# RWKV state exponentials: two clamps on GpSimd in place of two Relu passes on ScalarE, with a new order on all engines

## The chip, the cores and the metric

The kernel runs on one core of one Trainium2 chip. The metric is the device time of that core in microseconds, lower is better. The engines are called as in the profile: PE (TensorE, matrix multiplies), DVE (VectorE), ACT (ScalarE, the table functions), POOL (GpSimd) and SP (the queue that issues the transfers). Everything is float32.

## The reference

The input is 16 sequences of 512 tokens with 128 channels. Four blocks follow one another: a four-layer RWKV model with a residual, a feed-forward block with weights and activations rounded to FP4 in blocks of 16, a causal attention with one head, and the same feed-forward block again. Cut to what matters here:

```python
x = x + rwkv_model(_layernorm(x))      # 4 layers, each: time mix, then channel mix
x = x + fp4_ffn(_layernorm(x))
x = x + attention(_layernorm(x))
x = x + fp4_ffn(_layernorm(x))

def step(carry, kv):                   # the RWKV state, one token
    aa, bb, pp = carry
    kk, vv = kv
    ww = u + kk
    qq = jnp.maximum(pp, ww)
    e1 = jnp.exp(pp - qq)
    e2 = jnp.exp(ww - qq)
    out = (e1 * aa + e2 * vv) / (e1 * bb + e2)
    ww2 = pp + w                       # w = -exp(time_decay)
    qq2 = jnp.maximum(ww2, kk)
    e1b = jnp.exp(ww2 - qq2)
    e2b = jnp.exp(kk - qq2)
    return ((e1b * aa + e2b * vv, e1b * bb + e2b, qq2), out)
```

The two exponentials that carry the state forward are `e1b` and `e2b`. With `d = kk - pp` their arguments are `-relu(d - w)` and `-relu(w - d)`.

## The kernel before

Channels lie on the 128 partitions and the 512 tokens of one sequence along the free axis for the RWKV part, so one job is a 128x512 tile. There are 64 RWKV jobs `r` (4 layers by 16 sequences), 32 feed-forward jobs (16 for each of the two blocks) and 16 attention jobs. The running maximum, the denominator and the numerator of the state are three scans along the tokens on DVE (`scan_pp`, `scan_bb`, `scan_aa`).

The program is a software pipeline written out by hand. Each engine has one loop over ticks `t`, and the body of the loop is a list of stage functions, each called with its own lag, such as `exp_k(t - 6)`. A function does nothing when its job number is outside the range. So the order of one engine's instructions is that of its list, an engine works strictly in that order, and semaphores hold an instruction until what it reads has been made or what it overwrites has been read. Nothing else sets the order. A steady RWKV tick carries one instance of each RWKV stage, for some thirteen different jobs at once. RWKV jobs enter in ticks 0 to 63. `FFN_AT`, `ATT_AT` and `FFN2_AT` are the ticks in which the first feed-forward, attention and second feed-forward jobs enter: 69, 85 and 97 (`GAP` is 12). In the ticks in which attention and the second feed-forward overlap, both kinds of stage run.

The stages that the change touches, in job `r`: `scan_pp` makes the running maximum from the keys in PSUM, `sub_d` (DVE, L331) makes `d`, `args` (ACT, L818 and L819) makes both Relu arguments in `ed`, `exp_d` (L825) turns the first into a decay factor in PSUM bank T, `exp_k` (L830) turns the second into the weight of the new key, and `mul_s1`, `scan_bb`, `scan_aa` on DVE use them. Then POOL adds (`add_den` L649, `add_num` L655), ACT makes the seed of a reciprocal (`seeds`, L841), POOL multiplies (`scaled_p` L666, `mul_y` L660), and DVE finishes (`mul_u`, `rwkv`). POOL also makes the roots of the layer norms (`rsqrts`, L601 to L606) and differences of neighbouring tokens (`sub_dh1` L643, `sub_dh` L673), and adds the channel mix to `X` (`add_xb` L678). In a steady tick POOL runs eleven instructions. Six instructions of DVE in a tick read two tiles of SBUF: `mix_t` L307, `mix_rt` L314, `mix_k` L404, `mix_r` L411, `gated` L381 and `rwkv` L387.

## Time and profile before

| what | value |
|---|---|
| three runs, median (lowest to highest) | 1396.85 us (1396.58 to 1397.21) |
| profiled execution, span | 1396.8 us |
| PE busy | 1311.6 us, 94% |
| ACT busy | 1261.8 us, 90% |
| DVE busy | 1250.5 us, 90% |
| POOL busy | 1160.8 us, 83% |
| mean granted TensorE clock | 0.989 |

The span of the profiled execution is its own time from the first to the last instruction, and it stands at the median of the runs, so sums made against the span need no conversion. The shares of busy time are means over very different stretches: up to about 855 us the RWKV ticks, then the first feed-forward, from about 1106 us attention alone, from about 1180 us attention and the second feed-forward together, and from about 1279 us the second feed-forward alone. An instruction's duration in the trace holds some latency under which its successor already starts, so the time that an instruction takes from its engine is the distance from its start to the next start; such distances are called spacings below.

### The profile page before, as it was taken

The numbers are of one execution on the slowest core, as the hardware profiler recorded it, in microseconds if no ns is written. First come the engines' busy times: TensorE is split into PE (matmuls) and PEld (weight loads), VectorE is DVE, ScalarE is ACT, GpSimd is POOL, SyncE is SP. The second block draws the span as 40 slices with busy tenths as digits, with TensorE's granted clock in tenths as the row PEclk, the third lists the DMA queues.
The fourth block names the chain that finished last, engine by engine and source line by source line (L and its number), as shares of the span: only waits on it lengthen the run. The fifth ranks groups of instructions, "written<-read, shape, count | busy, mean of one in ns | idle before, by whom it ended". The sixth has DMA issues, their size and how long they took to land.

```text
span 1396.8 us, 23610 instructions
## 1 busy us (share of the span) xinstructions
PE 1311.6 (94%) x7285; PEld 929.9 (67%) x7285; DVE 1250.5 (90%) x2169; ACT 1261.8 (90%) x2533; POOL 1160.8 (83%) x1218
## 2 busy tenths in 40 slices
PE   3699999999999999999999999999999999999997
PEld 1356667666666666676666677766667777667776
DVE  6999999999999999999999999579999467789994
ACT  6799999999999999999999999767777889888874
POOL 6888999999998999998998999969998445467983
PEclk9999999999999999999999999999999999999999
DMA  7000000000000000000000000100000000000011
GB/s 232 0 1 1 1 1 1 1 20 13 1 1 1 1 1 1 1 1 1 1 2 0 1 1 9 31 24 23 24 1 1 1 1 1 1 8 23 24 31 38
DMA packets 26924, 18.55 MB, mean 13 GB/s; under 512 B 1072, under 2 KB 26160, under 8 KB 26800
## 3 DMA queue, kind: packets, MB, share of 16 engines
q1 hardware_dynamic: 26800, 17.05, 4.2%
q8 instruction: 59, 0.97, 0.3%
q14 instruction: 65, 0.53, 0.1%
HBM read 12.85 MB, written 4.19 MB: 12 GB/s over the span
## 4 chain that ended last, share of the span: by engine, by line
ACT 40%; PE 30%; issue 11%; POOL 10%; DVE 8%; DMA 0%; ACTq 0%; SPq 0%; POOLq 0%; DVEq 0%
ACT z L757 10%; ACT kf L867 6%; PE ps L1211 5%; ACT kf L874 3%; PE ps L1190 3%; ACT rc L841 3%; PE ps L1152 3%; ACT ed L818 3%; PE ps L1183 3%; PE ps L1261 3%; PE ps L1135 3%; ACT er L835 2%; PE ps L1243 2%; ACT ed L819 2%; ACT ed L830 2%
## 5 line engine op out<-in xcount | busy, mean ns | idle before, releaser
L1152 PEld LDWEIGHTS ps<-W,kf 128*128 128x128 f32 x2048 | 245.9, 193 | 33.1 <-issue 32.3
L1135 PE MATMUL ps<-xk,W 128*128 128x512 f32 x512 | 262.5, 595 | 1.0 <-DVE xk L404 0.9
L1152 PE MATMUL ps<-W,kf 128*128 128x128 f32 x2048 | 251.2, 276 | 0.0
L757 ACT ACTIVATE z<-X,ln_rs 128x128 f32<-128x128 f32 x512 | 219.2, 720 | 6.1 <-POOL ln_rs L606 6.1
L867 ACT ACTIVATE kf<-ps 128x512 f32<-128x512 f32 x256 | 210.8, 823 | 3.5 <-PE ps L1135 3.5
L874 ACT ACTIVATE kf<-kf 128x1024 f32<-128x1024 f32 x128 | 164.7, 1287 | 0.0
L1040 PEld LDWEIGHTS ps<-idn,z 128*128 128x128 f32 x664 | 81.1, 143 | 113.7 <-issue 68.4
L1040 PE MATMUL ps<-idn,z 128*128 128x128 f32 x664 | 101.9, 277 | 32.8 <-ACT z L757 19.4
L604 POOL TENSOR_TENSOR ln_rs<-ln_rs,mhalf 128x8 f32<-128x8 f32 (+1 forms) x70 | 122.9, 1756 | 0.0
L707 POOL TENSOR_TENSOR W<-W,hsc 128x704 f32<-128x704 f32 x64 | 88.9, 1389 | 30.3 <-DVE hsc L482 30.3
L666 POOL TENSOR_TENSOR p<-p,rc 128x512 f32<-128x512 f32 x64 | 104.2, 1628 | 8.6 <-DVE p L381 8.0
L673 POOL TENSOR_TENSOR dh<-h 128x512 f32<-128x512 f32 x64 | 66.8, 1044 | 48.4 <-ACT h L860 48.2
L1190 PE MATMUL ps<-WU,d 128*128 128x352 f32 x256 | 99.9, 472 | 5.5 <-DVE W L463 4.8
L1183 PE MATMUL ps<-WG,d 128*128 128x352 f32 x256 | 97.6, 463 | 0.6 <-ACT d L898 0.6
L358 DVE TENSOR_TENSOR_SCAN bb<-ps,ed 128x512 f32<-128x512 f32 x64 | 78.3, 1223 | 19.5 <-ACT ed L830 19.4
L713 POOL TENSOR_TENSOR W<-W,hsc 128x704 f32<-128x704 f32 x64 | 88.8, 1388 | 2.6 <-DVE W L494 2.5
L226 DVE BATCH_NORM_STATS2 ln_st<-X 128x6 f32<-128x256 f32 x256 | 90.5, 413 | 0.1
L1122 PEld LDWEIGHTS ps<-W,rc 128*128 128x128 f32 x512 | 67.0, 191 | 33.8 <-issue 33.8
L1142 PEld LDWEIGHTS ps<-W,xc 128*128 128x128 f32 x512 | 64.3, 191 | 36.5 <-ACT sr L810 24.8
L649 POOL TENSOR_TENSOR er<-er,bb 128x512 f32<-128x512 f32 x64 | 81.4, 1273 | 2.3 <-DVE bb L358 2.3
L655 POOL TENSOR_TENSOR rv<-rv,aa 128x512 f32<-128x512 f32 x64 | 81.5, 1273 | 1.4 <-DVE aa L366 1.3
L678 POOL TENSOR_TENSOR X<-X,cr 128x512 f32<-128x512 f32 x64 | 81.5, 1273 | 0.0
(178 smaller groups left out, 4041.5 us busy)
## 6 DMA issues: line engine op xcount, KB each, us to landing
X<-x_in SPq DMA_DIRECT2D x16, 256.0 KB, 6.8
xi<-x_in SPq DMA_DIRECT2D x16, 256.0 KB, 2.8
out<-X SPq DMA_DIRECT2D x16, 256.0 KB, 2.3
W<-weights SPq DMA_DIRECT2D x4, 832.0 KB, 8.4
W<-fp4w SPq DMA_DIRECT2D x1, 560.0 KB, 3.6
row<-rows SPq DMA_DIRECT2D x1, 192.0 KB, 2.9
wqkv<-qkv SPq DMA_DIRECT2D x1, 96.0 KB, 5.9
idn<-ident SPq DMA_DIRECT2D x1, 64.0 KB, 3.0
```

The costliest lines, as they stand in the source:

```text
L226: last = e.bn_stats(g.of(g.st, n)[:, 2 * k:2 * k + 2, :].rearrange("p a s -> p (a s)"), src[:, k * 256:(k + 1) * 256].rearrange("p (a c) - ...
L604: e.tensor_tensor(rs[:, 0, :], rs[:, 2, :], mhalf[:, 0:k], ALU.pow).then_inc(*own.next())
L666: e.tensor_tensor(p[r % 2][:, :], p[r % 2][:, :], rc[r % 2][:, :], ALU.mult).then_inc(ps_done, 1)
L707: e.tensor_tensor(h, h, spread(hsc[n % 2][:, 0, k * 44:(k + 1) * 44], 44), ALU.mult).then_inc(fh_y[k], 1)
L757: last = e.activation(chunk(dst, j), chunk(src, j), ACT.Identity, bias=rs[:, 1, j:j + 1], scale=rs[:, 0, j:j + 1])
L867: e.activation(kf[r % 3][:, f, :], (pF0, pF1)[f % 2][:, :], ACT.Relu).then_inc(relu_done[f], 1)
L874: e.activation(both, both, ACT.Square).then_inc(sq_done[k], 1)
L1040: last = e.transpose(chunk(dst, j), chunk(src, j), idn[:, :])
L1135: e.matmul((pF0, pF1)[f % 2][:, :], w_of(r, WCK + f), xk[r % 2][:, :], start=True, stop=True).then_inc(kf_mm[f], 1)
L1152: last = e.matmul(chunk(pKV, j), kf[r % 3][:, f, j * 128:(j + 1) * 128], w_of(r, WCV + f), start=f == 0 and j == 0, stop=f == 3, skip_grou ...
L1183: e.matmul(pG[j % 2][:, 0:I], chunk(fx[n % 2], j), WG[:, :], start=True, stop=True).then_inc(g_mm, 1)
L1190: e.matmul(pU[j % 2][:, 0:I], chunk(fx[n % 2], j), WU[:, :], start=True, stop=True).then_inc(u_mm, 1)
```

## The change

ACT no longer makes the arguments. `args` is gone, and POOL gets two functions. `clamp_old` writes `max(d, -ew)` (`ew` is `exp(time_decay)`, `wneg` its negative), `clamp_new` writes `min(d, -ew)`. The second operation of each is there only because the form takes two, with a bound of 3e38. The two exponentials now add the constant back as a bias read per partition: `exp(-(max(d, -ew)) - ew)` and `exp(min(d, -ew) + ew)`. One semaphore for the arguments becomes two. Arithmetic, tiles, matmuls and transfers are otherwise the same.

```diff
+FAR = 3e38
...
-GAP = 12
-ATT_AT, FFN2_AT, TICKS = FFN_AT + NB, FFN_AT + NB + GAP, FFN_AT + 2 * NB + GAP + 18
+ATT_AT, FFN2_AT = FFN_AT + 16, FFN_AT + 33
+TICKS = FFN2_AT + 35
...
             def sub_d(r):
                 if 0 <= r < NR:
-                    w.wait_ge(args_done, r - 1)
+                    w.wait_ge(old_done, r - 1)
+                    w.wait_ge(new_done, r - 1)
...
+            def clamp_old(r):
+                if 0 <= r < NR:
+                    w.wait_ge(wneg_done, 1)
+                    w.wait_ge(ed_done, r - 1)
+                    w.wait_ge(d_done, r + 1)
+                    e.tensor_scalar(ed[r % 2][:, 0, :], dd[r % 2][:, :], FAR, col(wneg, r), ALU.min, ALU.max).then_inc(old_done, 1)
+
+            def clamp_new(r):
+                if 0 <= r < NR:
+                    w.wait_ge(wneg_done, 1)
+                    w.wait_ge(s1_done, r - 1)
+                    w.wait_ge(bb_done, r - 1)
+                    w.wait_ge(d_done, r + 1)
+                    e.tensor_scalar(ed[r % 2][:, 1, :], dd[r % 2][:, :], col(wneg, r), -FAR, ALU.min, ALU.max).then_inc(new_done, 1)
...
-            def args(r):
-                if 0 <= r < NR:
-                    w.wait_ge(wneg_done, 1)
-                    w.wait_ge(s1_done, r - 1)
-                    w.wait_ge(bb_done, r - 1)
-                    w.wait_ge(d_done, r + 1)
-                    e.activation(ed[r % 2][:, 0, :], dd[r % 2][:, :], ACT.Relu, bias=col(ew, r))
-                    e.activation(ed[r % 2][:, 1, :], dd[r % 2][:, :], ACT.Relu, bias=col(wneg, r), scale=-1.0).then_inc(args_done, 1)
-
...
-                    w.wait_ge(args_done, r + 1)
-                    e.activation(pT[:, :], ed[r % 2][:, 0, :], ACT.Exp, scale=-1.0).then_inc(ed_done, 1)
+                    w.wait_ge(old_done, r + 1)
+                    e.activation(pT[:, :], ed[r % 2][:, 0, :], ACT.Exp, bias=col(wneg, r), scale=-1.0).then_inc(ed_done, 1)
...
-                    w.wait_ge(args_done, r + 1)
-                    e.activation(ed[r % 2][:, 1, :], ed[r % 2][:, 1, :], ACT.Exp, scale=-1.0).then_inc(ek_done, 1)
+                    w.wait_ge(new_done, r + 1)
+                    e.activation(ed[r % 2][:, 1, :], ed[r % 2][:, 1, :], ACT.Exp, bias=col(ew, r)).then_inc(ek_done, 1)
...
             for t in range(TICKS):
-                add_num(t - 7)
...
+                rsqrts(t - 2)
+                scaled_p(t - 6)
...
```

The four lists of stages, on DVE, POOL, ACT and PE, are all written anew, with other lags. `FFN_AT` and `ATT_AT` keep their values, 69 and 85; `FFN2_AT` goes from 97 to 102.

POOL, one steady RWKV tick of the program before. `dh` is both differences, `er` and `rv` the denominator and the numerator, `p` the gated output, `ln_rs` the roots:

```order
L673 TENSOR_TENSOR dh<-h 128x512
L601 TENSOR_SCALAR ln_rs<-ln_st 128x8
L602 TENSOR_SCALAR ln_rs<-ln_st 128x8
L604 TENSOR_TENSOR ln_rs<-ln_rs,mhalf 128x8
L606 TENSOR_TENSOR ln_rs<-ln_rs 128x8
L666 TENSOR_TENSOR p<-p,rc 128x512
L660 TENSOR_TENSOR er<-er,rc 128x512
L678 TENSOR_TENSOR X<-X,cr 128x512
L643 TENSOR_TENSOR dh<-h 128x512
L649 TENSOR_TENSOR er<-er,bb 128x512
L655 TENSOR_TENSOR rv<-rv,aa 128x512
```

POOL, the steady tick of the changed program, from the denominator on. L660 and L652 are the clamps:

```order
L666 TENSOR_TENSOR er<-er,bb 128x512
L672 TENSOR_TENSOR rv<-rv,aa 128x512
L660 TENSOR_SCALAR ed<-d,wneg 128x512
L652 TENSOR_SCALAR ed<-d,wneg 128x512
L690 TENSOR_TENSOR dh<-h 128x512
L603 TENSOR_SCALAR ln_rs<-ln_st 128x8
L604 TENSOR_SCALAR ln_rs<-ln_st 128x8
L606 TENSOR_TENSOR ln_rs<-ln_rs,mhalf 128x8
L608 TENSOR_TENSOR ln_rs<-ln_rs 128x8
L683 TENSOR_TENSOR p<-p,rc 128x512
L645 TENSOR_TENSOR dh<-h 128x512
```

Thirteen instructions stand in a tick where eleven stood. The clamps come straight ahead of the channel-mix difference and the roots, and behind the numerator.

DVE, the part of the steady tick with the instructions that read two tiles of SBUF, before:

```order
L373 SCALAR_TENSOR_TENSOR p<-ps,p 128x512
L331 TENSOR_TENSOR d<-ps,pp 128x512
L387 SCALAR_TENSOR_TENSOR rc<-er,p 128x512
L314 SCALAR_TENSOR_TENSOR sr<-dh,vec,h 128x512
L337 TENSOR_SCALAR er<-d,vec 128x512
L411 SCALAR_TENSOR_TENSOR xc<-dh,vec,h 128x512
L404 SCALAR_TENSOR_TENSOR xk<-dh,vec,h 128x512
L381 SCALAR_TENSOR_TENSOR p<-sr,rv 128x512
L307 SCALAR_TENSOR_TENSOR xt<-dh,vec,h 128x512
```

The same part of the changed program:

```order
L333 TENSOR_TENSOR d<-ps,pp 128x512
L375 SCALAR_TENSOR_TENSOR p<-ps,p 128x512
L227 BN_STATS ln_st<-X 128x6 x2
L389 SCALAR_TENSOR_TENSOR rc<-er,p 128x512
L383 SCALAR_TENSOR_TENSOR p<-sr,rv 128x512
L339 TENSOR_SCALAR er<-d,vec 128x512
L406 SCALAR_TENSOR_TENSOR xk<-dh,vec,h 128x512
L308 SCALAR_TENSOR_TENSOR xt<-dh,vec,h 128x512
L315 SCALAR_TENSOR_TENSOR sr<-dh,vec,h 128x512
L413 SCALAR_TENSOR_TENSOR xc<-dh,vec,h 128x512
```

The six still stand together with one other instruction among them. Between `d` and the first of them there are now two instructions, where there was none.

ACT, where the second feed-forward meets attention, in the program before. `er` is the SiLU of the feed-forward, `big` and `kf` with `sm` the exponentials of the softmax. The last such place but one:

```order
L983 ACTIVATE kf<-ps 128x384
L941 ACTIVATE X<-ps 128x512
L976 ACT_TABLE_LOAD
L976 ACTIVATE big,sm<-ps,sm 128x128
L983 ACTIVATE kf<-ps 128x256
```

The changed program where the first SiLU of the second feed-forward comes:

```order
L776 ACTIVATE z<-X,ff_rs 128x128 x4
L987 ACTIVATE big,sm<-ps,sm 128x512
L917 ACT_TABLE_LOAD
L917 ACTIVATE er<-ps 128x352
L994 ACTIVATE kf<-ps 128x512
```

Over the whole program the table loads go from 14 to 4: the last softmax exponential now stands ahead of the first SiLU of the second feed-forward, and they no longer alternate.

## Rows read from the trace of the kernel before

**Rows 1.** Busy time by engine in two stretches: 40 RWKV ticks, and attention overlapping feed-forward.
```profile
core 0: us, PE busy (x) PEld busy (x) DVE busy (x) ACT busy (x) POOL busy (x), PEclk, DMA share, GB/s
177.90:705.70 527.80, 527.25 (x2879) 361.75 (x2878) 510.15 (x801) 527.80 (x1001) 482.59 (x442) 1.00 0.01 3
...
1180.00:1279.00 99.00, 89.73 (x518) 65.75 (x519) 79.70 (x181) 84.24 (x187) 57.89 (x64) 1.00 0.02 6
```

**Rows 2.** Timeline of POOL: start, duration, then idle time before in brackets.
```profile
407.20 1.04 POOL L673 TENSOR_TENSOR dh<-h 128x512 f32<-128x512 f32 x1 [0.90 <-ACT h L860]
...
420.40 1.04 POOL L673 TENSOR_TENSOR dh<-h 128x512 f32<-128x512 f32 x1 [0.90 <-ACT h L860]
421.52 0.52 POOL L601 TENSOR_SCALAR ln_rs<-ln_st 128x8 f32<-128x8 f32 x1
422.12 0.62 POOL L602 TENSOR_SCALAR ln_rs<-ln_st 128x8 f32<-128x8 f32 x1
422.71 1.85 POOL L604 TENSOR_TENSOR ln_rs<-ln_rs,mhalf 128x8 f32<-128x8 f32 x1
424.64 0.39 POOL L606 TENSOR_TENSOR ln_rs<-ln_rs 128x8 f32<-128x8 f32 x1
425.05 1.72 POOL L666 TENSOR_TENSOR p<-p,rc 128x512 f32<-128x512 f32 x1
```

**Rows 3.** Timeline of ACT in the same tick, around the two argument passes.
```profile
422.26 0.97 ACT L867 ACTIVATE kf<-ps 128x512 f32<-128x512 f32 x1
422.74 1.10 ACT L818 ACTIVATE ed<-d,ew 128x512 f32<-128x512 f32 x1
423.35 1.10 ACT L819 ACTIVATE ed<-d,wneg 128x512 f32<-128x512 f32 x1
423.96 1.16 ACT L803 ACTIVATE h<-ps,vec 128x512 f32<-128x512 f32 x1
```

**Rows 4.** Longest wait of PE's weight loads beside a matmul group, 200 to 800 us.
```profile
PEld ps L1142 <- ACT sr L810: 24.3, 39, 0.7
```

**Rows 5.** POOL groups: shape and count, then busy us, mean ns.
```profile
L707 POOL TENSOR_TENSOR W<-W,hsc 128x704 f32<-128x704 f32 x64 | 88.9, 1389 | 30.3 <-DVE hsc L482 30.3
...
L655 POOL TENSOR_TENSOR rv<-rv,aa 128x512 f32<-128x512 f32 x64 | 81.5, 1273 | 1.4 <-DVE aa L366 1.3
...
L694 POOL TENSOR_TENSOR z<-z,xsc 128x512 f32<-128x512 f32 x22 | 23.6, 1075 | 16.3 <-DVE xsc L442 16.3
...
L601 POOL TENSOR_SCALAR ff_rs<-ff_st 128x4 f32<-128x4 f32 x32 | 6.3, 197 | 8.2 <-DVE ff_st L226 5.6
```

**Rows 6.** Timeline of DVE in the tick of rows 2 and 3: first two, last.
```profile
421.24 0.74 DVE L387 SCALAR_TENSOR_TENSOR rc<-er,p 128x512 f32<-128x512 f32 x1
421.90 0.74 DVE L314 SCALAR_TENSOR_TENSOR sr<-dh,vec,h 128x512 f32<-128x512 f32 x1
...
424.89 0.74 DVE L307 SCALAR_TENSOR_TENSOR xt<-dh,vec,h 128x512 f32<-128x512 f32 x1
```

**Rows 7.** Timeline of DVE: the same line in two neighbouring ticks, later.
```profile
721.29 0.68 DVE L393 TENSOR_TENSOR X<-X,ps 128x512 f32<-128x512 f32 x1
...
733.80 0.68 DVE L393 TENSOR_TENSOR X<-X,ps 128x512 f32<-128x512 f32 x1
```

**Rows 8.** Timelines of DVE and ACT: ticks of attention, of both, of feed-forward.
```profile
1139.82 1.13 DVE L527 SCALAR_TENSOR_TENSOR X<-ps,sm,X 128x128 f32<-128x128 f32 x4 [1.07 <-PE ps L1261]
1147.50 1.13 DVE L527 SCALAR_TENSOR_TENSOR X<-ps,sm,X 128x128 f32<-128x128 f32 x4 [0.41 <-PE ps L1261]
...
1222.71 1.11 DVE L527 SCALAR_TENSOR_TENSOR X<-ps,sm,X 128x128 f32<-128x128 f32 x4
1238.66 1.12 DVE L527 SCALAR_TENSOR_TENSOR X<-ps,sm,X 128x128 f32<-128x128 f32 x4
...
1297.98 0.60 ACT L941 ACTIVATE X<-ps 128x512 f32<-128x512 f32 x1
1307.87 0.60 ACT L941 ACTIVATE X<-ps 128x512 f32<-128x512 f32 x1
```

**Rows 9.** ACT groups: table loads of the softmax exponential and of SiLU.
```profile
L906 ACT ACT_TABLE_LOAD x7 | 9.0, 1283 | 5.7 <-PE ps L1183 5.7
L976 ACT ACT_TABLE_LOAD x6 | 7.7, 1283 | 0.1
```

More of the change, by code:

```diff
@@ L573, in vector @@
[L573 to L584 removed]
+                mix_r(t - 12)
+                mul_rv(t - 7)
+                fh_add(ffn_job(t - 8), 0)
@@ new lines, in vector @@
+                mul_up(ffn_job(t - 7), 3)
+                mul_s1(t - 7)
+                fh_sub(ffn_job(t - 8), 0)
+                fh_max(ffn_job(t - 7))
+                scan_bb(t - 7)
+                scan_aa(t - 7)
+                a_add(att_job(t - 9))
+                fh_add(ffn_job(t - 8), 1)
+                fh_scale(ffn_job(t - 7))
+                fx_max(ffn_job(t - 3))
+                fh_inverse(ffn_job(t - 7))
+                add_xa(t - 9)
+                gate(t - 13)
+                mul_up(ffn_job(t - 6), 0)
@@ new lines, in vector @@
+                fh_sub(ffn_job(t - 8), 1)
+                scan_pp(t - 6)
+                prepare(t - 4)
+                a_mask(att_job(t - 7), 0)
+                bn2(t - 9)
+                sub_d(t - 6)
+                a_max(att_job(t - 7), 0)
+                a_mask(att_job(t - 7), 1)
+                fx_scale(ffn_job(t - 3))
+                weights_scales(t - Q_AT + 4)
+                a_max(att_job(t - 7), 1)
+                f_bn(ffn_job(t))
+                mul_u(t - 8)
+                bn1(t - 3)
@@ new lines, in vector @@
+                rwkv(t - 8)
+                a_inverse(att_job(t - 8))
+                a_mask(att_job(t - 7), 2)
+                mul_up(ffn_job(t - 6), 1)
+                gated(t - 7)
+                arg_r(t - 6)
+                a_max(att_job(t - 7), 2)
+                init_stats(t - 1)
+                mix_k(t - 10)
+                mix_t(t - 5)
+                a_mask(att_job(t - 7), 3)
+                fx_add(ffn_job(t - 4))
+                mix_rt(t - 5)
+                a_bn(att_job(t - 3))
@@ new lines, in scalar @@
+                put_x(ffn_job(t - 8))
+                f_z(ffn_job(t - 1))
+                tanh_c(t - 11)
+                init_z(t - 1)
+                seeds(t - 6)
+                a_exp(att_job(t - 6), 3)
+                exp_k(t - 5)
+                exp_r(t - 5)
+                keep_h1(t - 3)
+                relu(t - 10, 3)
+                silu(ffn_job(t - 4), 0)
+                a_z(att_job(t - 3))
+                exp_d(t - 5)
+                keep_av(att_job(t - 5))
+                fh_magic(ffn_job(t - 6), 1)
@@ new lines, in scalar @@
+                keep_hq(ffn_job(t - 7), 1)
+                keep_hq(ffn_job(t - 7), 0)
+                tanh_r(t - 5)
+                norm2(t - 8)
+                weights_out(t - Q_AT - 14)
+                keep_x(ffn_job(t - 8))
+                norm1(t - 2)
+                relu(t - 9, 0)
+                keep_pt(att_job(t - 6), 0)
+                square(t - 10, 0)
+                square_1(t - 6)
+                keep_pt(att_job(t - 6), 1)
+                relu(t - 9, 1)
+                a_exp(att_job(t - 5), 0)
@@ new lines, in tensor @@
+                ff_keys(t - 11, 3)
+                turn1(t - 4)
+                lend_M(ffn_job(t - 6), 0)
+                h_turn(ffn_job(t - 8), 0)
+                ff_values(t - 12, 1)
+                receptance(t - 6)
+                h_turn(ffn_job(t - 8), 1)
+                lend_T(t - 6)
+                down(ffn_job(t - 9))
+                similarity(att_job(t - 6), 0)
+                h_turn(ffn_job(t - 8), 2)
+                lend_M(ffn_job(t - 6), 1)
+                p_turn(att_job(t - 7), 0)
```

226 lines of the change are left out of this document (71 added, 155 removed).

## The prediction

> **What bounds the kernel now.** I read the busy time by stretch first, because the shares over the whole span mix four kinds of work. Over 40 steady RWKV ticks (527.80 us, so 13.20 us each) ACT is busy for all of the stretch and PE for all but half a microsecond, DVE has about 0.44 us idle in a tick and POOL about 1.13 us [rows 1]. Then I read the timelines of one such tick. POOL repeats after 13.20 us with one idle piece of 0.90 us ahead of the channel-mix difference, so its list takes 12.30 us as it stands [rows 2]. ACT starts one pass as the spacing of the last is over: it is the bound, and its list is 13.20 us long. PE is close behind it. Its busy time is modelled, so I look at what its weight loads wait for: those of L1142 wait for ACT 39 times, 24.3 us, or 0.62 us a tick [rows 4], part of it under the matmul ahead. So PE's own list lies between 12.6 and 13.2 us; I take 13.1, since its busy row shows almost no hole. DVE's own list I read where it has fallen behind and runs without a hole: 12.51 us from tick to tick [rows 7]. So the four lists are, in order, ACT 13.2, PE 13.1, DVE 12.5, POOL 12.3. Whatever shortens ACT alone can give 0.1 us a tick before PE ends it, and POOL has room for 0.9 us.
>
> **What goes from ACT.** The two argument passes have spacings of 0.61 us each, 1.22 us a tick [rows 3]. The two exponentials get a bias per partition. No row shows an exponential with and without one; the bound is nothing from below, and from above the difference between the biased Relu (0.61) and the unbiased Relu of L867 (0.48), 0.13 us each. I take the upper end, since the nearest row is also an ACT pass over 512 columns: ACT falls to 13.20 - 1.22 + 0.26 = 12.2 us a tick and is no longer a bound.
>
> **What comes to POOL.** Two clamps a tick. The trace has no one-input POOL instruction on 512 columns, so this is the cost to bound. From below: a one-input instruction on 4 columns takes 0.197 us, which is nearly all fixed cost [rows 5]. From above: the two-input addition on the same shape, 1.27 us long, with a spacing of some 1.24. Between them, the products with a spread factor are 1.389 us for 704 columns and 1.075 for 512 [rows 5], so 0.314 us for 192 columns, 1.64 ns a column for two inputs. If a POOL instruction is paced by what it reads, one input costs half of that, 0.42 us for 512 columns, and with the fixed 0.2 the clamp takes about 0.6 us. I take 0.60; the ends 0.20 and 1.24 stay for the range.
>
> The Trainium skill says on this, in "GPSIMD Engine Reference", section 3.1, that a body of one or two operations runs at 1.03 cycles an element, and that the best a general loop has shown is 768 ns for 512 elements. The first would give 0.44 us plus the fixed part, the second 0.77 us plus it; no row here shows either. By the second the sum would be some 0.35 us a tick worse than mine.
>
> POOL's list becomes 12.30 + 2 x 0.60 = 13.50 us, if it loses as much to DVE as now. That is 0.30 us more than the tick of before. The idle 0.90 us [rows 2] covers three quarters of the clamps and the rest is on the path, because POOL then never rests. I count 51 ticks in which this holds: the 40 of [rows 1] and 11 more up to 855 us. 51 x 0.30 = 15.3 us more.
>
> **What POOL loses to DVE.** POOL and DVE side by side show a second cost [rows 2, 6]. The first root instruction L601 takes 0.52 us here and the same line takes 0.197 us on half the columns in the feed-forward. It starts at 421.52, while DVE's L387, which reads two tiles of SBUF, runs to 421.98, and it ends just after that. L602 (0.62) ends as DVE's L314 ends. The product L666 takes 1.72 us against 1.27 for its like L655; it starts under DVE's L307. So POOL waits while DVE reads two SBUF tiles: 0.32 for L601, about 0.4 for L602, 0.45 for L666, and a little in the others, some 1.5 us of its 12.3. What keeps this small is where the six such DVE instructions stand: from 421.24 to 425.6 they lie over the roots, which read eight columns.
>
> The Trainium skill states a rule for this, in "SBUF — State Buffer", section "Who interferes with whom": a DVE instruction with two SBUF inputs and a POOL instruction that reads SBUF share a read interface, and the one that comes first holds it to its end. The trace agrees on POOL's side (1.72 against 1.27). The rule speaks against this change, because each clamp is one more SBUF read on POOL.
>
> In the new order the clamps can't start before `d`, and behind `d` DVE has only `mul_u` and a pair of statistics, about 1.25 us, before the six begin. POOL needs 2 x 0.60 + 1.0 for the clamps and the difference L690 before it is at the roots. So the roots come about 1 us after the six have begun, and one or two of these fall on a POOL instruction with 512 columns. Bounds: the loss falls by all of its 1.5 us, or the first two of the six add their length, 0.6 each, to it. I take no difference, since the roots still lie under four of the six.
>
> **The other waits.** `clamp_new` waits for `d`; behind it on POOL stand the other clamp, the difference and the roots, for which ACT's two norms and then PE's transposes wait. If `d` is late all of that is late, but POOL, as the bound, should be late itself. The exponentials have most of a tick until DVE needs them. `sub_d` waits for the clamps of two jobs back and never does. These I cost at nothing; if they are not hidden, each gap on POOL is worth its length in every tick. Matmuls and transfers are the same in number and kind, and SP's queue is untouched.
>
> **The opening.** Ticks of before with the input norm in them are longer. ACT gets 1 us a tick there but PE has the mixes of the first ten jobs as further matmuls and POOL its clamps. Between 5 us gained and 5 lost over those ticks; I take 2 gained.
>
> **The tail.** Ten of 14 table loads go; at 1283 ns each [rows 9] that is 12.8 us of ACT. A tick of attention alone takes 7.68 us, a tick of both 15.95, and a tick of feed-forward alone 9.89 [rows 8]. Overlapping saves 7.68 + 9.89 - 15.95 = 1.6 us for each pair, and the changed program gives up some five such pairs, 8 us lost. Against it stand the emptying and filling ticks between the two, which are shorter than full ones, and the table loads: PE is busy for 89.73 of 99 us in the overlap [rows 1], so up to 9.3 us can be got back there. The ends are 8 us lost and 12.8 gained; I take 5 us gained, since ACT's loads stand on the way of SiLU, for which DVE waits.
>
> **Sum.** Against the span of 1396.8 us, which is the median of the runs (1396.85): 1396.8 + 15.3 - 2 - 5 = 1405.1 us.
>
> **Rivals.**
> - *The clamps fit (faster).* If two clamps take no more than POOL's idle 0.9 us, or the loss to DVE falls by 0.3 us or more, PE is the bound at 13.1. For it: the order keeps the six DVE instructions together, as it would have to. Against it: it needs 0.45 us a clamp, hardly more than half the reading of a two-input product with almost no fixed part. Time: 1396.8 - 51 x 0.1 - 2 - 5 = 1384.7 us. Chance 0.30.
> - *The cost cancels.* A tick of 13.3 to 13.35 us, 51 x 0.13 = 6.6 us, is what the opening and the tail give. Time: 1396.4 us. Chance 0.12.
> - *POOL and DVE take turns (much slower).* The clamps and L690 fall under the first two of the six and push the roots out from under the rest. It decides once POOL starts a 512-column read later than about 1 us after `d`. Both wait in turn, 0.6 us more a tick: 51 x 0.9 = 45.9 us, time 1396.8 + 45.9 - 7 = 1435.7 us. For it: the 1 us above, and that DVE's own slack is only 0.7 us. Chance 0.12.
> - *A clamp costs what a two-input addition does.* POOL at 12.30 + 2 x 1.24 = 14.78, 51 x 1.58 = 80.6 us, time 1470 us. Chance 0.04.
> - The forecast, POOL the bound at 13.50 us: chance 0.42, with its own range of 1397 to 1418 us (13.35 to 13.75 a tick).
>
> **How the numbers follow.** A measurement of this kernel tells 0.2%, 2.8 us, from no change. Faster is the first rival and a little of the second, 0.31. Within 0.2% is most of the second and the low edge of the forecast, 0.13. The rest is slower, 0.56. The range must hold eight in ten and cases of both signs: it starts at 1384, the first rival's own time, which leaves out some 0.12 for an opening and a tail that give their most, and ends at 1436, the time of the rival of turns, which leaves out the last rival and a little more, about 0.08.
>
> **What would show it.** In the steady ticks of the changed profile: the tick by POOL's starts should be 13.5 us with no idle piece on POOL, the clamps about 0.64 us long, 0.60 in spacing; ACT should be idle for about 1.3 us a tick; the difference ahead of the roots may be longer than 1.04 us. In the tail, 4 table loads, and attention ticks of 7.7 us up to the end of attention. The forecast is wrong if POOL shows idle time in the steady ticks, if the tick is at or under 13.2 us, or if a clamp is over 0.8 us long.

## The result and the profile after

The changed kernel takes 1443.06 us (median of 4 runs, 1441.99 to 1443.67) against 1396.71 us of the kernel before on the same chip: 1.033 times as long, interval 1.0316 to 1.0345. The forecast was 1405 us, the range ended at 1436. The direction was right and the size was not.

The span went from 1396.8 to 1442.3 us, 45.5 us more. I cut it by the starts of DVE's residual addition (L393 before, L395 after), which stands once in each of the 64 RWKV jobs:

| stretch | before | after | difference |
|---|---|---|---|
| start to the 13th addition | 217.25 | 238.50 | +21.3 |
| 13th to 46th, 33 steady ticks | 435.68 | 452.86 | +17.2 |
| 46th to 64th, in which the second set of weights is prepared | 231.74 | 249.91 | +18.2 |
| 64th to the end | 512.1 | 501.0 | -11.1 |

A steady tick is 13.72 us, 0.52 more than before. Over the 51 steady ticks of the prediction that is 26.6 us; 21.3 lie in the opening, some 9 between the 46th and the 64th addition on top of the steady ticks' own 0.52, and the tail gave 11.1 back.

The first view is the busy time by engine, from the page and for 480 us of steady ticks (35 of them), to be set beside [rows 1].

```profile
PE 1332.3 (92%) x7285; PEld 944.6 (65%) x7285; DVE 1328.8 (92%) x2169; ACT 1194.5 (83%) x2395; POOL 1258.0 (87%) x1346
```

```profile
core 0: us, PE busy (x) PEld busy (x) DVE busy (x) ACT busy (x) POOL busy (x), PEclk, DMA share, GB/s
211.06:691.36 480.30, 466.93 (x2522) 323.90 (x2521) 480.30 (x701) 429.28 (x806) 470.92 (x456) 1.00 0.01 3
```

ACT has come off the bound (1.46 us idle a tick), as intended. DVE is busy for 480.30 of 480.30 us and POOL seems to have 0.27 us a tick free. Both readings mislead. POOL's 0.27 us is the time between the end of one record and the start of the next, none of it a wait; and DVE fills its time only because some of its instructions are long. The timelines show it. First POOL, one steady tick, the answer to [rows 2]: start, duration, and no idle piece in brackets anywhere.

```profile
415.81 1.26 POOL L677 TENSOR_TENSOR er<-er,rc 128x512 f32<-128x512 f32 x1
...
419.49 1.28 POOL L672 TENSOR_TENSOR rv<-rv,aa 128x512 f32<-128x512 f32 x1
420.88 0.68 POOL L660 TENSOR_SCALAR ed<-d,wneg 128x512 f32<-128x512 f32 x1
421.56 0.69 POOL L652 TENSOR_SCALAR ed<-d,wneg 128x512 f32<-128x512 f32 x1
422.21 1.47 POOL L690 TENSOR_TENSOR dh<-h 128x512 f32<-128x512 f32 x1
423.66 0.63 POOL L603 TENSOR_SCALAR ln_rs<-ln_st 128x8 f32<-128x8 f32 x1
424.37 0.35 POOL L604 TENSOR_SCALAR ln_rs<-ln_st 128x8 f32<-128x8 f32 x1
424.70 2.11 POOL L606 TENSOR_TENSOR ln_rs<-ln_rs,mhalf 128x8 f32<-128x8 f32 x1
426.89 0.45 POOL L608 TENSOR_TENSOR ln_rs<-ln_rs 128x8 f32<-128x8 f32 x1
427.30 1.27 POOL L683 TENSOR_TENSOR p<-p,rc 128x512 f32<-128x512 f32 x1
...
429.53 1.26 POOL L677 TENSOR_TENSOR er<-er,rc 128x512 f32<-128x512 f32 x1
```

The line repeats after 13.72 us. A clamp costs 0.68 and 0.65 us from start to start. The first also starts 1.39 us after L672, where such an addition otherwise takes 1.23, so there is 0.15 us more between the addition and the clamp. What makes it isn't shown: the same change of form, from a difference to a root instruction, had 1.12 us behind the 1.04 us long L673 in the kernel before, and has 1.45 behind the 1.47 us long L690 here. Two clamps take 0.68 + 0.65 + 0.15 = 1.48 us. [Rows 2] had 12.30 us of work; 12.30 + 1.48 = 13.78, and 13.72 was measured.

DVE beside it, the answer to [rows 6]:

```profile
421.75 1.04 DVE L389 SCALAR_TENSOR_TENSOR rc<-er,p 128x512 f32<-128x512 f32 x1
422.71 1.52 DVE L383 SCALAR_TENSOR_TENSOR p<-sr,rv 128x512 f32<-128x512 f32 x1
424.15 0.47 DVE L339 TENSOR_SCALAR er<-d,vec 128x512 f32<-128x512 f32 x1
```

L389 ends 0.54 us after the clamp L652 has ended (422.79 against 422.25), L383 0.55 us after the difference L690 (424.23 against 423.68): each waited for POOL's instruction and then ran. Undisturbed they take about 0.7 us, as in [rows 6]. Here it is DVE that waits for POOL, the other way round than in [rows 6]. L690 in turn takes 1.47 us where it took 1.04, and L683 takes 1.27 where its like took 1.72 [rows 2]: these two nearly cancel on POOL.

ACT in the same tick answers to [rows 3]; the second fence is the list of waits from 200 to 800 us (engine and line, whom it waits for, us in all, times, longest).

```profile
422.48 0.73 ACT L840 ACTIVATE ed<-ed,ew 128x512 f32<-128x512 f32 x1
424.66 0.63 ACT L845 ACTIVATE er<-er 128x512 f32<-128x512 f32 x1 [1.45 <-DVE er L339]
...
426.33 0.69 ACT L835 ACTIVATE ps<-ed,wneg 128x512 f32<-128x512 f32 x1
426.95 0.59 ACT L829 ACTIVATE sr<-ps 128x512 f32<-128x512 f32 x1
```

```profile
ACT er L845 <- DVE er L339: 61.5, 42, 2.5
...
PE ps L1095 <- DVE xt L308: 19.0, 42, 2.2
```

ACT and PE, the tightest two before, now wait in every tick; PE's wait for ACT of [rows 4] is gone. L835 has a spacing of 0.62 us with the bias; the same pass without one had 0.54 in the kernel before (L825), and so has L831, shown under the order alone below. So the bias costs 0.08 us. The prediction said that no row shows this pair, but the trace of the kernel before has it: the seeds' exponential L841 reads a bias and has a spacing of 0.61 us.

### The profile page after: what moved, and what is told of

It reads as the page before. It is cut to its first block, busy times and chain, and to the rows that moved or that the text cites. A ratio compares the mean times of both kernels' runs of the same rounds, so it can differ in the third digit from the quotient of the medians.

```text
span 1442.3 us, 23756 instructions
## 1 busy us (share of the span) xinstructions
PE 1332.3 (92%) x7285; PEld 944.6 (65%) x7285; DVE 1328.8 (92%) x2169; ACT 1194.5 (83%) x2395; POOL 1258.0 (87%) x1346
## 4 chain that ended last, share of the span: by engine, by line
DVE 41%; PE 27%; POOL 15%; issue 13%; ACT 3%; DVEq 0%; DMA 0%; POOLq 0%; SPq 0%; ACTq 0%
PE ps L1221 5%; DVE aa L368 4%; DVE pp L324 4%; PE ps L1200 4%; PE ps L1193 3%; DVE ln_st L227 3%; DVE rc L389 3%; PE ps L1209 3%; DVE p L383 3%; PE ps L1253 2%; PE ps L1271 2%; POOL ln_rs L606 2%; DVE rv L346 2%; DVE sr L315 2%; DVE xk L406 2%
## 5 line engine op out<-in xcount | busy, mean ns | idle before, releaser
L776 ACT ACTIVATE z<-X,ln_rs 128x128 f32<-128x128 f32 x512 | 204.3, 488 | 21.2 <-POOL ln_rs L608 21.2
L877 ACT ACTIVATE kf<-ps 128x512 f32<-128x512 f32 x256 | 150.3, 587 | 3.1 <-PE ps L1145 2.8
L606 POOL TENSOR_TENSOR ln_rs<-ln_rs,mhalf 128x8 f32<-128x8 f32 (+1 forms) x70 | 136.1, 1944 | 0.0
L884 ACT ACTIVATE kf<-kf 128x1024 f32<-128x1024 f32 x128 | 135.1, 1057 | 0.0
L1145 PEld LDWEIGHTS ps<-xk,W 128*128 128x128 f32 x512 | 88.3, 194 | 65.9 <-issue 59.4
L845 ACT ACTIVATE er<-er 128x512 f32<-128x512 f32 x64 | 40.3, 630 | 79.3 <-DVE er L339 79.3
L690 POOL TENSOR_TENSOR dh<-h 128x512 f32<-128x512 f32 x64 | 89.1, 1393 | 0.1
L917 ACT ACTIVATE er<-ps 128x352 f32<-128x352 f32 x128 | 58.7, 458 | 36.8 <-PE ps L1193 21.6
L383 DVE SCALAR_TENSOR_TENSOR p<-sr,rv 128x512 f32<-128x512 f32 x64 | 86.6, 1353 | 0.0
L683 POOL TENSOR_TENSOR p<-p,rc 128x512 f32<-128x512 f32 x64 | 85.0, 1328 | 0.0
```

The lines of the kernel that those rows point to most:

```text
L383: e.scalar_tensor_tensor(out=p[r % 2][:, :], in0=sr[r % 3][:, :], scalar=1.0, in1=rv[r % 2][:, :], op0=ALU.add, op1=ALU.mult).then_inc(p_d ...
L606: e.tensor_tensor(rs[:, 0, :], rs[:, 2, :], mhalf[:, 0:k], ALU.pow).then_inc(*own.next())
L690: e.tensor_tensor(dh2[r % 2][:, :], h2[r % 2][:, 1:T + 1], h2[r % 2][:, 0:T], ALU.subtract).then_inc(dh2_done, 1)
L776: last = e.activation(chunk(dst, j), chunk(src, j), ACT.Identity, bias=rs[:, 1, j:j + 1], scale=rs[:, 0, j:j + 1])
L877: e.activation(kf[r % 3][:, f, :], (pF0, pF1)[f % 2][:, :], ACT.Relu).then_inc(relu_done[f], 1)
L884: e.activation(both, both, ACT.Square).then_inc(sq_done[k], 1)
```

## The experiments

Theory A said that POOL and DVE wait for each other in the steady tick and that this ring sets 13.72 us. Theory B said that POOL's list is simply too long and DVE has slack for its own waits. Beside these stood the question what the new order is worth without clamps, and how the opening lost 21 us. "Opening" is the stretch up to the 13th addition and "tail" the one behind the 64th, as in the table; a plus is time lost against the kernel before. The ratios stand with their 95% intervals, against the kernel before on the same chip.

**The new order alone.** The changed lists, with the arguments still on ACT.

```diff
-                clamp_new(t - 4)
-                clamp_old(t - 4)
...
+                args(t - 5)
                 exp_k(t - 5)
```

> The changed kernel with its new lists, but both arguments made again by the two Relu passes on ACT (ahead of exp_k) and no clamps on POOL. Steady tick of the changed kernel: 13.72 us with DVE never idle. Theory A (DVE waits behind POOL): the difference L690 then starts right behind the numerator and is over before the six two-tile instructions of DVE begin, DVE falls back to 12.5 us, ACT's 13.2 us is the bound, and the tail keeps the 11 us that the changed kernel won there: about 1386 us. Theory B (POOL's list is too long by the clamps, 12.30 + 2 x 0.67 = 13.63): the same 13.2 us a tick. Theory C (the new order is bad by itself): the tick stays at 13.5 us or more and the time over 1410 us.

Measured: 1404.31 us, 1.0061 (1.0045 to 1.0076). A miss. The tick is 13.34 us, the 13th addition comes at 228.1 us (+10.9), the stretch from the 46th to the 64th is 3.9 us longer, and the tail is 498.6 us (-13.5). ACT in a steady tick:

```profile
422.26 0.73 ACT L820 ACTIVATE ed<-d,wneg 128x512 f32<-128x512 f32 x1
423.02 0.63 ACT L831 ACTIVATE ed<-ed 128x512 f32<-128x512 f32 x1
423.56 0.61 ACT L836 ACTIVATE er<-er 128x512 f32<-128x512 f32 x1
```

The second argument pass has a spacing of 0.76 where it had 0.61 [rows 3], because the exponential behind it reads its result at once: moved away from it (the mended order below), the pass has 0.61 again. So about half of the opening's loss belongs to the order, and the tail's gain is the order's.

**Short clamps.** The changed kernel with clamps on 8 of 512 columns; the exponentials read `d` with a scale of 0, so it leaves out the use of the clamped values. `sub_d` also waits for these exponentials, since they now read `d`; the trace shows no wait of `sub_d`.

```diff
-  e.tensor_scalar(ed[r % 2][:, 0, :], dd[r % 2][:, :], FAR, col(wneg, r), ALU.min, ALU.max)
+  e.tensor_scalar(ed[r % 2][:, 0, 0:8], dd[r % 2][:, 0:8], FAR, col(wneg, r), ALU.min, ALU.max)
...
-  e.activation(pT[:, :], ed[r % 2][:, 0, :], ACT.Exp, bias=col(wneg, r), scale=-1.0)
+  e.activation(pT[:, :], dd[r % 2][:, :], ACT.Exp, bias=col(wneg, r), scale=0.0)
```

> The changed kernel with both clamps on 8 of 512 columns, and the two exponentials fed from d with scale 0 (they no longer use the clamped values, so this part of the computation is left out). POOL's list gets about 0.9 us shorter a tick, the order of every engine is the same. Theory B (sum of POOL's list): the tick falls from 13.72 to PE's 13.1 or 13.2 us, 51 x 0.55 = 28 us, time 1415 us or less. Theory A (where POOL's 512-column instruction L690 stands against DVE's first two-tile instructions): if L690 moves out from under them DVE's L383 is 0.7 us again and the tick is 13.2; if POOL, no longer late, still starts L690 just after d, L383 keeps 1.0 us or more and the tick stays over 13.4 us, time over 1428 us.

Measured: 1402.83 us, 1.0043 (1.003 to 1.0057). POOL and PE:

```profile
275.30 0.26 POOL L662 TENSOR_SCALAR ed<-d,wneg 128x8 f32<-128x8 f32 x1
275.55 0.27 POOL L654 TENSOR_SCALAR ed<-d,wneg 128x8 f32<-128x8 f32 x1
275.78 1.03 POOL L692 TENSOR_TENSOR dh<-h 128x512 f32<-128x512 f32 x1
...
419.15 1.04 POOL L692 TENSOR_TENSOR dh<-h 128x512 f32<-128x512 f32 x1 [0.18 <-ACT h L872]
```

```profile
305.70 1.02 PE L1119 MATMUL ps<-sr,W 128*128 128x512 f32 x2
...
318.80 1.02 PE L1119 MATMUL ps<-sr,W 128*128 128x512 f32 x2
```

For the first ticks DVE's additions come every 12.88 us, at the pace of POOL without a gap, and then every 13.10. PE does 13.10 from its first steady tick: it had run ahead, that lead was used up, and then it is the bound. So PE's own list is 13.10 us, and POOL's with clamps of 8 columns is 12.88.

The steady ticks lose nothing with these clamps, but the opening does: the 13th addition comes at 232.9 us, 15.6 late, where the order alone has 10.9 and the changed kernel 21.3. So 4.7 of the 10.4 us that the clamps add there don't come from their length. That leaves the clamps' place in POOL's list: POOL stands still there until `d` is made, 8 times in this kernel's opening, 13.0 us in all, and what follows on POOL meets other instructions of DVE, which are 4.2 us longer in sum than with the order alone (22.0 against 17.8, by the count given with the roots below). That is a reading of the traces; no run separates the two. In the stretch around the second set of weights it is the same: 237.6 us, 5.9 more than before, though a steady tick is shorter than before's.

**Clamps of 256 columns.** The kernel of the last experiment, with the same part left out.

```diff
-  e.tensor_scalar(ed[r % 2][:, 0, 0:8], dd[r % 2][:, 0:8], FAR, col(wneg, r), ALU.min, ALU.max)
+  e.tensor_scalar(ed[r % 2][:, 0, 0:256], dd[r % 2][:, 0:256], FAR, col(wneg, r), ALU.min, ALU.max)
```

> The short-clamp kernel with 256 of 512 columns in each clamp (the exponentials again do not use the clamped values). With 8 columns the tick was 12.93 to 13.05 (PE), with 512 it is 13.72. If POOL's list sets the tick (theory B), it follows the clamp's length: 0.47 us over 504 columns is 0.93 ns a column, so two halves less is 0.48 us less: 13.25 us a tick, 1443 - 51 x 0.48 = 1419 us. If where the instructions meet sets it (theory A), a jump instead of the middle: 13.0 or 13.7.

Measured: 1421.42 us, 1.0178 (1.0164 to 1.0191), the tick 13.32, near the 13.25 of theory B; the 13th addition comes at 236.0 us.

```profile
426.28 0.47 POOL L662 TENSOR_SCALAR ed<-d,wneg 128x256 f32<-128x256 f32 x1
426.74 0.47 POOL L654 TENSOR_SCALAR ed<-d,wneg 128x256 f32<-128x256 f32 x1
```

The duration of a clamp goes 0.26, 0.47, 0.68 us over 8, 256 and 512 columns, and POOL's tick 12.88, 13.32, 13.72. POOL's list sets the tick.

**`d` earlier on DVE.** The changed kernel, with the gate and a statistics pair behind `d` instead of ahead of it.

```diff
-                gate(t - 13)
...
-                bn2(t - 9)
                 sub_d(t - 6)
+                gate(t - 13)
+                bn2(t - 9)
```

> The changed kernel with two functions moved in DVE's list: sub_d goes from behind bn2 to straight behind scan_pp, and gate goes behind it, so 2.5 us instead of 1.26 stand between the start behind d and the first instruction that reads two tiles (L389). Nothing else moves. Theory A (DVE waits behind POOL's clamp_old and L690): POOL can take the clamps up to 1.2 us earlier, L383 falls from 1.52 to about 0.7 us and L389 from 1.04 to 0.7, DVE is no longer the bound, and the tick falls to what POOL's list then takes, 13.4 to 13.6 us: 1443 - 51 x 0.2 = 1433 us, and more where ticks were long in the opening. Theory B (POOL's list alone sets the tick): POOL has no idle time to win, the tick stays at 13.72 and the time at 1443 us.

Measured: 1439.87 us, 1.0304 (1.029 to 1.0318), the tick 13.72 as before this edit. Theory A fell. The busy times over the same stretch:

```profile
211.06:691.36 480.30, 468.69 (x2524) 318.98 (x2523) 475.63 (x701) 430.12 (x806) 470.93 (x456) 1.00 0.01 3
```

DVE shows 4.67 us idle and the tick doesn't move, while POOL's 470.93 us is unchanged to a hundredth. A DVE without a hole was not the bound. The turn itself was not taken away by this edit, since L383 still takes 1.52 us and L690 still 1.47; what it shows is that DVE has time to spare for its side of it.

**The root of the input norm beside the other roots.** The changed kernel, one line moved in POOL's list.

```diff
                 rsqrts(t - 2)
+                init_rsqrt(t)
...
-                init_rsqrt(t)
```

> The changed kernel with one line moved in POOL's list: init_rsqrt from behind mul_y to straight behind rsqrts. It only acts in the first ticks, in which the input norm runs. In these the changed kernel is 21 us behind the one before (start of the 13th addition L395 at 238.5 us against 217.3). If that comes from DVE's row of eight two-tile instructions (the six and the two of init_affine) meeting POOL's 512-column reads at its end, four more small instructions on POOL under that row take L297 and L413 from 1.6 and 1.5 us back to 0.7: 5 to 10 us less by the 13th addition, and 1433 to 1438 us. If it comes from the length of the lists, nothing changes.

Measured: 1436.93 us, 1.0281 (1.0266 to 1.0297). The steady tick is the same, the 13th addition comes at 232.7 us instead of 238.5. Four instructions on 4 columns, moved, gave 5.8 us. What they had pushed, in the opening of the changed kernel:

```profile
172.98 2.36 POOL L683 TENSOR_TENSOR p<-p,rc 128x512 f32<-128x512 f32 x1
175.30 1.48 POOL L645 TENSOR_TENSOR dh<-h 128x512 f32<-128x512 f32 x1
```

```profile
174.25 1.64 DVE L297 TENSOR_TENSOR X<-xi,row 128x512 f32<-128x512 f32 x1
175.81 1.52 DVE L413 SCALAR_TENSOR_TENSOR xc<-dh,vec,h 128x512 f32<-128x512 f32 x1
```

These are turns: a product on POOL of 2.36 us where 1.27 is its undisturbed time, then L297 of 1.64 and L413 of 1.52 us on DVE, each ending about 0.55 us after one of POOL's. In the opening they cost. That DVE is busy for 182.1 of 184.5 us from 54 us to the 13th addition (before: 160.2 of 163.3) would not prove it, as the steady tick teaches; but here POOL does wait, and always for DVE's `d`:

```profile
POOL ed L660 <- DVE d L333: 10.0, 7, 2.2
```

I summed what each DVE instruction there takes beyond the shortest of its function and shape in that stretch: 5.3 us before, 23.1 after, 17.8 with the new order alone and 22.0 with it and clamps of 8 columns. The 17.8 us more stand against 21.3 us lost. So turns can account for most of the loss; this one edit shows 5.8 us of it.

**One clamp, order of before.** The kernel before, the old-state clamp on POOL behind the channel-mix difference, the other argument on ACT.

```diff
                 sub_dh(t - 10)
+                clamp_old(t - 6)
...
-                    e.activation(ed[r % 2][:, 0, :], dd[r % 2][:, :], ACT.Relu, bias=col(ew, r))
```

> The kernel before, its order unchanged, with the first argument made by one clamp on POOL (behind the channel-mix difference, ahead of the roots) and the second still by one Relu on ACT. POOL's list 12.30 + 0.67 = 12.97 us, ACT's 13.20 - 0.61 + 0.13 = 12.7, so by lists PE's 13.1 us is the bound: 1396.7 - 51 x 0.1 = 1391.6 us. By theory A the clamp runs when DVE's first two-tile instruction (L387) wants the port: DVE loses up to 0.6 us (12.5 to 13.1) and the roots are pushed 0.67 us later, so a tick of 13.1 to 13.6 us and 1392 to 1417 us.

Measured: 1400.2 us, 1.0024 (1.0014 to 1.0033). The tick falls by 0.10 us to 13.10, ticks of 12.87 and 13.32 in turn, which is PE's 13.10 in the mean. By lists alone 1391.6 us was expected; the time lies in the range given for theory A. POOL in two neighbouring ticks:

```profile
423.40 1.00 POOL L651 TENSOR_SCALAR ed<-d,wneg 128x512 f32<-128x512 f32 x1
...
436.37 1.56 POOL L651 TENSOR_SCALAR ed<-d,wneg 128x512 f32<-128x512 f32 x1 [0.23 <-DVE d L332]
```

The clamp that takes 0.68 us in the changed kernel takes 1.00 or 1.56 here, by what DVE runs beside it. The opening (+3.3) and the stretch from the 46th to the 64th addition (+3.6) lost more than the 3.4 us that the 33 steady ticks and the 1.5 that the tail gained.

**One clamp in the new order.** The new order with roots together and the clamp behind the difference.

```diff
                 sub_dh(t - 8)
+                clamp_old(t - 4)
...
-                    e.activation(ed[r % 2][:, 0, :], dd[r % 2][:, :], ACT.Relu, bias=col(ew, r))
```

> The order-only kernel (new lists, both arguments on ACT, 1404.3 us) with clamp_old back on POOL, behind the difference L690 instead of ahead of it, clamp_new still a Relu on ACT, and init_rsqrt moved behind rsqrts. By lists ACT has 13.2 - 0.61 + 0.08 = 12.7, POOL 12.30 + 0.67 = 12.97, PE 12.9 as the run with short clamps showed. If the two-tile instructions stay clear of POOL the tick is 13.0 instead of 13.34: 51 x 0.3 = 15 us, and the opening gives 5: 1385 us. If the clamp, which now comes last ahead of the roots, pushes them out from under the six (theory A), the tick is 13.3 to 13.5 and the time 1400 us or more.

Measured: 1401.32 us, 1.0027 (1.0018 to 1.0037). By lists 1385 us was expected, so this is a miss. The tick is 13.20 and the clamp 1.52 us long, under L389 and L383, with POOL never idle. With the clamp ahead of the difference the tick is 13.07 (one clamp, mended, below). So in this place the turns do lengthen POOL's list, by 0.13 us a tick.

**A later start of the second feed-forward alone.** The kernel before with `GAP = 17`.

```diff
-GAP = 12
+GAP = 17
```

> The kernel before with one number changed, GAP 17 for 12, so the second feed-forward starts five ticks later against attention. The changed kernel's stretch behind the last RWKV addition to X was 11 us shorter than that of before. If the later start made that: 1385.7 us (1382 to 1389) and 4 table loads. If the new lists made it: 1397 us or up to 1405, since five overlapped pairs at 15.95 become pairs at 17.6 us.

Measured: 1401.72 us, 1.0037 (1.0024 to 1.0049). A miss: the table loads fall from 14 to 4, and the tail is still 2.9 us longer.

**Old RWKV lists, new lists behind them.** The kernel before up to the feed-forward and the changed one after it; the diff is against the changed kernel.

```diff
-FFN_AT = NR + 5
+FFN_AT = NR + 7
...
-                mix_r(t - 12)
-                mul_rv(t - 7)
+                mix_rt(t - 6)
+                arg_r(t - 6)
```

> RWKV, input norm and weight stages in the list of before with their lags and the Relu passes on ACT; the feed-forward and attention stages stand behind them in the order and lags of the new lists, and enter two ticks later (FFN_AT 71), since earlier they would wait for each other in a ring. It asks whether the 11 to 13.5 us that the new lists win behind the last RWKV addition come with the stages' own order. The RWKV ticks as before (13.2 us). If the order makes it and the two later ticks cost nothing, 1384 us; two more emptying ticks of about 8 us each and the simple order while both kinds run would bring it to 1395 to 1410 us.

Measured: 1406.5 us, 1.0061 (1.0048 to 1.0075). Another miss: RWKV is as before (last addition at 884.56 us) and the tail takes 519.4 us. From the last addition to the first one of attention it needs 231.2 us, where the kernel before has 221.7 and the changed one 213.1. Behind that addition it takes 288.3 us, as the changed kernel (287.9; before 290.4). So the 2.5 us there go with the attention and feed-forward lists themselves. For the hand-over this run gives no answer: the feed-forward enters two ticks later than in the changed kernel, at some 8 us a tick by the expectation's own estimate, which can be most of the 18.1 us.

**The order, mended.** The new order alone, with the three places changed that the traces had named: the input norm's root beside the others, `weights_rounded` earlier on DVE, the arguments further from their exponential.

```diff
+                weights_rounded(t - Q_AT - 4)
...
+                init_rsqrt(t)
...
+                args(t - 5)
```

> The order-only kernel (both Relu passes on ACT, no clamps, new lists) with three lines moved: init_rsqrt behind rsqrts on POOL, weights_rounded behind arg_r on DVE (it stood at the end of the row of two-tile instructions, where its tick took 20 us), args one place earlier on ACT, ahead of seeds, so that the first exponential no longer waits 0.15 us for them. Theory: the new order's own loss was the opening (10.9 us by the 13th addition), the weights tick (about 6) and that 0.15 us; its gain the tail (13.5). Mended: opening 5, weights 0 to 2, a tick of 13.20, tail -13.5: 1388 to 1392 us. If these lengths come from elsewhere: 1402 us or more.

Measured: 1395.2 us, 0.9993 (0.9984 to 1.0002): no change against before, and 3 us above the expected range. The tick is 13.20, the opening +5.0 and the tail 499.1 us, as expected. The tick of the weights takes 23.1 us, where it took 20.1 with the order alone, so that move made it worse. The steady tick is ACT's list again: POOL waits for ACT as in [rows 2].

```profile
424.71 1.03 POOL L674 TENSOR_TENSOR dh<-h 128x512 f32<-128x512 f32 x1 [0.91 <-ACT h L861]
```

**One clamp, mended.** The last kernel with `clamp_old` ahead of the channel-mix difference.

```diff
+                clamp_old(t - 4)
                 sub_dh(t - 8)
...
-                    e.activation(ed[r % 2][:, 0, :], dd[r % 2][:, :], ACT.Relu, bias=col(ew, r))
```

> As the mended order-only kernel, but with clamp_old on POOL ahead of the difference (its place in the changed kernel) and clamp_new still a Relu on ACT. In the order-only kernel POOL stands idle for 1.04 us exactly there, waiting for ACT's h2. One clamp costs 0.75 us of POOL (1.49 for the two in the changed kernel), so POOL's list is 12.30 + 0.75 = 13.05 us, ACT's 12.7, PE's 12.9: a tick of 13.05, 0.15 less than with none: 1389 - 51 x 0.15 = 1382 us. If the clamp pushes the roots from under the two-tile instructions as in the run with the clamp behind the difference (13.20 and 1401 us), 1390 us or more.

Measured: 1397.79 us, 1.001 (1.0001 to 1.0018). The tick is 13.07, as expected, and the total is a miss: the opening takes 2.1 us more than without the clamp and the stretch of the weights 5.3 us more. Here the clamp costs POOL its least:

```profile
422.67 1.29 POOL L664 TENSOR_TENSOR rv<-rv,aa 128x512 f32<-128x512 f32 x1
424.08 0.69 POOL L652 TENSOR_SCALAR ed<-d,wneg 128x512 f32<-128x512 f32 x1
```

0.65 us and again the 0.15 or so ahead of it. POOL's list with one clamp is 13.07, with two 13.72 us: the second costs its 0.65.

**Both clamps, mended.** The changed kernel with the root and the weights moved the same way.

```diff
+                weights_rounded(t - Q_AT - 4)
...
+                init_rsqrt(t)
```

> The changed kernel, both clamps on POOL, with init_rsqrt and weights_rounded moved as in the mended order-only kernel. Steady ticks stay at 13.72 us, since POOL's list is the same. The opening gives 6 us (as the run that moved init_rsqrt alone) and the weights tick up to 6: 1430 to 1434 us. The distance to the mended order-only kernel is then what two clamps cost with the order held: about 41 us.

Measured: 1436.57 us, 1.0286 (1.027 to 1.0302). It differs from the mended order by the clamps in place of the argument passes: 41.4 us. By stretch that is 10.4 in the opening, 17.4 in the 33 steady ticks, 11.6 from the 46th to the 64th addition (9.5 of them at the 0.53 us of a steady tick) and 2.1 in the tail. The distance was expected at 41 us; the time itself is 3 us above the expected range, because moving `weights_rounded` gave next to nothing (the root alone had given 1436.93 us).

## Why the prediction came out wrong

**What bounds the kernel.** Right. ACT's list is 13.20 us: it sets the tick of the mended order too. PE's is 13.10, as taken: with short clamps PE repeats after 13.10 us without a break, and one clamp in before's order gives 13.10 in the mean.

**ACT's part.** Right in kind. ACT is 1.46 us idle a tick (forecast 1.3). The bias costs 0.08 us, not the upper end 0.13.

**The size of a clamp: the first term that was mis-sized.** The prediction said "I take 0.60", 1.20 for two; measured are 1.48 with the 0.15 ahead of them. POOL's list of 12.30 was right to 0.1 us (12.88 less 2 x 0.25 for the short clamps and 0.15 leaves 12.23), that POOL never rests was right, and a tick of 13.72 lay at the edge of the forecast's own 13.35 to 13.75. The excess over 13.20 was 0.52 instead of 0.30, over 51 ticks 26.6 instead of 15.3 us: 11.3 us of the 38 that the forecast was short. (The opening adds 23.3 to that, the stretch around the weights some 9, and the tail takes 6.1 off.) The Trainium skill's first figure ("GPSIMD Engine Reference", section 3.1), 0.44 us and the fixed part of some 0.2, was nearer (by estimate 0.64 us, measured 0.68) than its general loop of 0.77 and more; the slope agrees too, 0.21 us for 256 columns, 0.82 ns a column. The sentence that by the second figure the sum would be some 0.35 us a tick worse was added up wrongly: 2 x (0.77 + 0.2 - 0.60) is 0.74 us.

**The opening: the step that failed.** The prediction said "between 5 us gained and 5 lost over those ticks; I take 2 gained". It was 21.3 us lost. I had priced the engines' added and removed work there, and nothing for turns. But there the input norm puts further reads of two tiles on DVE and roots on POOL; DVE's instructions are 17.8 us longer in all, and POOL, which has no wait in the steady ticks, waits for `d` for 10.0 us, so that DVE's length counts. The runs split the loss: 10.9 us come from the order, 5.8 of these from the place of the input norm's roots, and 10.4 from the clamps, of which 4.7 are there with clamps of 8 columns too.

**What POOL loses to DVE.** "I take no difference" was right for the steady tick: L690 loses 0.43 us and L683 gains 0.45. It was taken for all 64 jobs, and doesn't hold for the ticks with more work in them. The longest of these prepares the second set of weights. DVE and POOL before, where POOL was waiting for DVE while DVE multiplied:

```profile
742.95 1.32 DVE L280 TENSOR_TENSOR W<-W 128x1120 f32<-128x1120 f32 x1
744.31 1.33 DVE L282 TENSOR_TENSOR W<-W 128x1120 f32<-128x1120 f32 x1
```

```profile
743.75 0.59 POOL L606 TENSOR_TENSOR ln_rs<-ln_rs 128x8 f32<-128x8 f32 x1
747.64 1.72 POOL L666 TENSOR_TENSOR p<-p,rc 128x512 f32<-128x512 f32 x1 [3.30 <-DVE p L381]
```

And after, where POOL has work at that time:

```profile
816.17 2.42 DVE L281 TENSOR_TENSOR W<-W 128x1120 f32<-128x1120 f32 x1
818.63 2.04 DVE L283 TENSOR_TENSOR W<-W 128x1120 f32<-128x1120 f32 x1
820.59 1.75 DVE L413 SCALAR_TENSOR_TENSOR xc<-dh,vec,h 128x512 f32<-128x512 f32 x1
```

```profile
817.38 2.12 POOL L645 TENSOR_TENSOR dh<-h 128x512 f32<-128x512 f32 x1
819.45 2.34 POOL L677 TENSOR_TENSOR er<-er,rc 128x512 f32<-128x512 f32 x1
```

That tick takes 21.1 us, before 16.7. These three DVE instructions take 6.2 us in place of 3.4. But this is the new order's doing and not the clamps': with the order alone the tick takes 20.1 us, and the same lines (L281 and L283) are as long.

```profile
787.06 2.04 DVE L281 TENSOR_TENSOR W<-W 128x1120 f32<-128x1120 f32 x1
789.14 2.28 DVE L283 TENSOR_TENSOR W<-W 128x1120 f32<-128x1120 f32 x1
```

What the clamps add there shows behind it. The next two ticks take 12.5 us each with the order alone, as they do before, and so make up for part of the long one; with the clamps they take 13.6 and 13.7, because POOL has no time left to catch up in. So of the some 9 us of that stretch most come only with the clamps, though not with their length: clamps of 8 columns lose nearly as much.

**The other waits.** "These I cost at nothing" held in the steady ticks. Outside them the clamp waits for `d`, as the prediction feared, 10.0 us in the opening. Not all of that is a loss: with the order alone POOL's roots wait there for DVE's statistics, 11.2 us. DVE's L406 waits for L690 behind the clamps 11 times, 11.0 us in all; its like before waited twice, 3.5 us.

**The tail.** Forecast 5 us gained, measured 11.1. The table loads did fall to four and attention ticks stay at 7.68 us:

```profile
L917 ACT ACT_TABLE_LOAD x2 | 2.6, 1283 | 0.0
```

```profile
1210.82 1.13 DVE L529 SCALAR_TENSOR_TENSOR X<-ps,sm,X 128x128 f32<-128x128 f32 x4 [1.21 <-PE ps L1271]
1218.50 1.13 DVE L529 SCALAR_TENSOR_TENSOR X<-ps,sm,X 128x128 f32<-128x128 f32 x4 [1.21 <-PE ps L1271]
```

But the reason given was wrong, so the right sign is luck. Without overlap and with old lists the part from the first addition of attention to the end takes 295.2 us against 290.4: giving up the overlap loses 4.8 us net, loads included. The gain is the order's: 287.9 us in that part, and 213.1 instead of 221.7 us from the last RWKV addition to attention (288.7 and 209.9 with the order alone).

**The rivals.** The rival of turns gave 1435.7 us, near the result, for another reason. Its trigger came: L690 starts 1.66 us after `d` ends and falls under L383. Its price did not, 0.9 us a tick against 0.52 measured, of which the turns have no part that can be seen: on POOL what L690 loses and L683 gains cancel, and on DVE, with `d` about 1 us ahead, the long L383 stayed and the tick did too, with DVE partly idle. The turns cost where I had not looked, outside the steady ticks. The clamps' fit failed by POOL's size alone: with one clamp the tick is 13.07 to 13.20 by its place, with two 13.72.

What stays open: how much of the opening's other 5 us of the order is turns and how much the lags, and how the 10.4 us that the clamps cost there divide into turns, the wait for `d` and POOL's longer list. That ACT's slack could be turned into a gain with one clamp isn't excluded either; the three kernels with one clamp came out between 1397.8 and 1401.4 us, and no kernel is below the one before by more than the interval.

## What to carry to other kernels

An engine that is busy in every tenth of a microsecond need not be the bound: if it shares a read path, its instructions stretch into its slack, and only moving or shortening work tells. Cost a shift to another engine in each kind of tick, not in the steady one alone: the clamps cost 0.53 us in a steady tick, and 10.4 us up to the 13th addition, 0.8 us a job. An engine that has just lost its slack also no longer catches up behind a long tick. A new order is tested alone before the edit that it was made for is judged: here it was worth -1 to +8 us by itself, against 39 to 41 for the edit.
